# A decoder layer on one core: how the context of a convolution gets reversed and turned

## What is computed

```python
x1 = layernorm(x + linear_attention(x))          # stage 1
# stage 2: k = v = context, q = x1, 512 features in heads of 8, L = positions x features by head
kv  = einsum('bhil,bhjl->bijhl', k_, v_)         # all pairs of a head's 8 rows
y   = irfft(rfft(kv) * rfft(ssm_kernel))[..., :L] + kv * D   # causal convolution along l
out = einsum('bijhl,bhil->bjhl', y, q_)
x2  = layernorm(x1 + out)
# stage 3: 4-bit weights, SiLU gate, 1408 hidden features
x3  = layernorm(x2 + rmsnorm(down(silu(gate(x2)) * up(x2))))
```

## Time and profile before

| what | value |
|---|---|
| device time, 3 runs | median 538.91 us (538.29 to 539.4) |
| the profiled execution's own time | 539.25 us |
| its span in the profile | 537.4 us, 11880 instructions |
| granted TensorE clock over the span | 0.995 of full speed |
| DMA, whole span | 66147 packets, 40.64 MB, mean 76 GB/s |

### The profile page before, as it was taken

How to read it: one execution, slowest core, us unless ns; L and a number is a source line. 1 busy time by engine, 2 the same in 40 slices (tenths; PEclk the granted TensorE clock), 3 DMA queues, 4 the chain that set the end, 5 groups by cost and what they waited for, 6 DMA issues and landing times.

```text
span 537.4 us, 11880 instructions
## 1 busy us (share of the span) xinstructions
PE 512.8 (95%) x3734; PEld 385.9 (72%) x3734; DVE 383.2 (71%) x1169; ACT 405.8 (76%) x962; POOL 393.7 (73%) x449
## 2 busy tenths in 40 slices
PE   6899999998998999999999999999999999999992
PEld 6788888776775678667767776777677767765661
DVE  2897679998787677876778677778777777763223
ACT  3468774338998888878888898889788877788981
POOL 2379694994798499859967995899589949871231
PEclk9999999999999999999999999999999999999998
DMA  9445584705414761132104110411041111001001
GB/s 225 102 119 124 132 169 108 183 1 123 135 53 86 143 132 51 49 86 93 55 7 112 63 59 0 117 59 59 5 116 35 39 29 51 1 1 41 1 21 39
DMA packets 66147, 40.64 MB, mean 76 GB/s; under 512 B 37882, under 2 KB 55418, under 8 KB 66106
## 3 DMA queue, kind: packets, MB, share of 16 engines
q1 hardware_dynamic: 66106, 40.13, 29.5%
HBM read 27.46 MB, written 12.66 MB: 75 GB/s over the span
## 4 chain that ended last, share of the span: by engine, by line
PE 44%; POOL 28%; issue 18%; DVE 4%; ACT 3%; POOLq 1%; DMA 1%; DVEq 0%; ACTq 0%
POOL shared L295 9%; POOL h_lo L1103 6%; PE p_qk L901 5%; POOL kv L195 3%; PE p_cv L867 3%; PE p_cv L135 3%; PE p_n L1296 3%; PE p_n L1294 3%; PE p_n L1295 3%; PE p_cv L137 3%; PE p_cv L136 3%; POOL shared L297 2%; PE p_n L912 2%; PE p_x L1281 2%; PE p_n L957 2%
## 5 line engine op out<-in xcount | busy, mean ns | idle before, releaser
L1103 POOL TENSOR_TENSOR h_lo<-w,h_hi 128x256 f16<-128x256 f32 x88 | 70.5, 807 | 46.9 <-ACT h_hi L1152 45.4
L135 PE MATMUL p_cv<-kv_hi,toe 128*128 128x288 f16 x320 | 91.6, 286 | 0.8 <-DVE shared L255 0.8
L136 PE MATMUL p_cv<-kv_lo,toe 128*128 128x288 f16 x320 | 91.5, 286 | 0.0
L137 PE MATMUL p_cv<-kv_hi,toe 128*128 128x288 f16 x320 | 91.5, 286 | 0.0
L1135 ACT ACTIVATE p_qk<-p_qk,rescale 128x256 f32<-128x256 f32 x192 | 78.3, 450 | 12.9 <-PE p_qk L1283 12.3
L1135 ACT ACTIVATE p_x<-p_x,rescale 128x256 f32<-128x256 f32 x192 | 78.4, 452 | 8.1 <-PE p_x L1283 8.0
L295 POOL TENSOR_TENSOR shared<-shared 128x1024 f32<-128x1024 f32 x32 | 75.5, 2360 | 4.9 <-DVE shared L255 4.9
L1135 ACT ACTIVATE p_s<-p_s,rescale 128x256 f32<-128x256 f32 x144 | 58.9, 455 | 10.9 <-PE p_s L1283 10.9
L1294 PE MATMUL p_n<-wd_hi,h_hi 128*128 128x512 f16 x176 | 66.8, 379 | 0.0
L1296 PE MATMUL p_n<-wd_hi,h_lo 128*128 128x512 f16 x176 | 66.7, 379 | 0.0
L1295 PE MATMUL p_n<-wd_lo,h_hi 128*128 128x512 f16 x176 | 66.7, 379 | 0.0
(11 more groups left out here) (170 smaller groups left out, 1283.7 us busy)
## 6 DMA issues: line engine op xcount, KB each, us to landing
toe<-toeplitz_rows SPq DMA_DIRECT2D x16, 512.0 KB, 3.7
cnat<-in_ctx SPq DMA_DIRECT2D x16, 256.0 KB
xq<-x_blocks SPq DMA_DIRECT2D x16, 256.0 KB, 6.0
xr<-x_rows SPq DMA_DIRECT2D x16, 256.0 KB
out_x<-fin SPq DMA_DIRECT2D x16, 256.0 KB
ring<-in_x SPq DMA_DIRECT2D x6, 512.0 KB, 4.8
x_rows<-ring SPq DMA_DIRECT2D x6, 512.0 KB, 3.5
x_blocks<-ring SPq DMA_DIRECT2D x48, 64.0 KB
```

The costliest lines, as they stand in the source:

```text
L135: nc.tensor.matmul(dst, hi, kh, start=(mb == 0), stop=False)
L136: nc.tensor.matmul(dst, hi, kl, start=False, stop=False)
L137: done = nc.tensor.matmul(dst, lo, kh, start=False, stop=(mb == lb))
L1103: nc.gpsimd.tensor_tensor(h_lo[:, i, :], h32[:, i % 2, :], h_hi[:, i, :], ALU.subtract).then_inc(h_low, 1)
```

## The change

- The context is copied once, early in the program, from its input into a second tensor in DRAM, `ctx_quarters`, in quarters of its columns (32 of every 128), batches grouped by parity. These are 40 DMAs from DRAM to DRAM, ten steps `cr0` to `cr9` of four on SP's queue (`quarter_ctx`); their runs are 32 numbers (128 bytes) long. Steps cr0 to cr3 bring 32 positions each of one parity, cr4 to cr9 bring 64.
- `cnat` is loaded from `ctx_quarters` with four DMAs of 64 KB in place of one of 256 KB (`load_ctx`, step `cx`). It waits until the copy steps of its positions have landed.
- ScalarE's steps `rv` and `ct`/`kt` and TensorE's step `ct`/`f` go. VectorE's new step `ct`/`kt` (`turn_ctx`) turns `cnat` in 32x32 blocks, read backwards, into `kT`.
- x1 is stored in quarters too: four DMAs a tile in place of eight, with runs of 32 numbers as before; `xq` is loaded in rows of 512 numbers instead of four rows of 128. `turn_q` writes in another pattern.
- All tables of the start and of the periods are new.

```diff
+def load_quarters(sp, dst, quarters, row, signal):
+    src = quarters[:, bass.ds(row, 16)].rearrange("f s e c x -> f (s e) (c x)")
+    sp.dma_start(dst[:], src).then_inc(signal, 16)
+
+def load_ctx(sp, dst, quarters, row, signal):
+    for c in range(4):
+        src = quarters[:, :, c, bass.ds(row, 16)].rearrange("f e s x -> (f e) s x")
+        sp.dma_start(dst[:, c * P:(c + 1) * P], src).then_inc(signal, 16)
...
+    def turn(dst, src, order, first, step):
+        return nc.vector.transpose(
+            bass.AP(dst.tensor, dst.offset, [list(dst.ap[0]), [16, 16]] + order),
+            bass.AP(src.tensor, src.offset + first, [list(src.ap[0]), [32, 4], [P, 4], [step, 32]]))
...
-        nc.vector.transpose(cv.qv[p][:].rearrange("p (e r j) -> p r e j", e=2, j=8),
-                            cv.xq[p][:].rearrange("p (b k c) -> p k b c", k=KD, c=32)).then_inc(cv.q_kept, 1)
+        turn(cv.qv[p][:], cv.xq[p][:], [[256, 2], [1, 8], [8, 2]], 0, 1).then_inc(cv.q_kept, 1)
+
+    def turn_ctx(g, p):
+        dve.wait_ge(cv.in_ctx[p], (g + 1) * 64)
+        wait(dve, cv.kv_made, (g - 1) * HG + 2 * p + 2)
+        turn(cv.kT[p][:], cv.cnat[p][:], [[8, 2], [256, 2], [1, 8]], 31, -1).then_inc(cv.kT_kept, 1)
...
+        def quarter_ctx(n):
+            r, e = n // 2, n % 2
+            rows = (slice(0, 32), slice(32, 64), slice(64, 128), slice(128, 192), slice(192, 256))[r]
+            for f in range(LB):
+                sp.dma_start(ctx_quarters[f, e, :, rows, :].rearrange("b s (k c) -> b s k c", c=32),
+                             ctx_in[e::2, rows, :].rearrange("b s (k f c) -> f b s k c", f=4, c=32)[LB - 1 - f]
+                             ).then_inc(ctx_quartered[r], 16)
...
             elif name == "cx":
-                sp.wait_ge(cv.ctx_reversed, i - 1)
-                load_ctx(g, p)
+                sp.wait_ge(ctx_quartered[(0, 1, 2, 2)[g]], 128)
+                if g > 0:
+                    sp.wait_ge(cv.kT_kept, i - 1)
+                load_ctx(sp, cv.cnat[p], ctx_quarters, g * 32 + p * 16, cv.in_ctx[p])
...
-    START_SYNC = ("cx2 x3 cx3 x4 st0 st1 tw0 x5 x6 st2 toe0 st3 cx4 xq0 xq1 xq3 toe1 xr0 x7 xq2 cx6 xr1 toe2 xr3 cx5 "
-                  "st4 xq5 toe3 xq4 xr2 toe4 st5 cx7 toe5 st6 st7").split()
+    START_SYNC = ("x3 cr0 cr1 cx1 cx0 cr2 x4 cr3 cx2 cr4 st0 tw0 x5 st1 toe0 toe1 x6 st2 st3 x7 xq0 cr5 xq2 xr0 xq1 "
+                  "toe2 st4 xq3 cx4 xr1 xq4 cr6 cx3 toe3 xr3 st5 cx6 cx5 cr7 xr2 xq5 cr8 toe4 toe5 st6 st7 cr9 cx7").split()
```

More of the change, by code:

```diff
@@ L153, in flip_x2 @@
         done.then_inc(cv.x2_flipped, 1)
-    return bank_after, flip_ctx, convolve, flip_r, flip_x2
+    return bank_after, convolve, flip_r, flip_x2
 def conv_on_scalar(nc, act, cv):
[L160 to L173, removed]
     def high_kv(g, h):
@@ L367, in first_stage @@
     in_x = [sem(f"in_x{k}") for k in range(RING)]
-    x1_blocked = [sem(f"x1_blocked{k}") for k in range(RING)]
+    x1_quartered = [sem(f"x1_quartered{k}") for k in range(RING)]
+    ctx_quartered = [sem(f"ctx_quartered{k}") for k in range(5)]
     x1_stored = [sem(f"x1_stored{k}") for k in range(RING)]
@@ L402, in load_x @@
             wait(sp, x1_stored[i % RING], 16 * (i // RING))
[L403 removed]
+            wait(sp, x1_quartered[i % RING], 64 * (i // RING))
             sp.dma_start(ring[i % RING][:], tokens(x, i)).then_inc(in_x[i % RING], 16)
@@ L408, in store_x1 @@
             sp.dma_start(tokens(x1_rows, i), ring[i % RING][:]).then_inc(x1_stored[i % RING], 16)
[L409 to L418, removed]
+            for f in range(LB):
+                sp.dma_start(x1_quarters[f, P * (i // 4):P * (i // 4) + P, :, i % 4].rearrange(
+                    "s e (k c) -> s e k c", c=32),
+                             ring[i % RING][:].rearrange("p e (k f c) -> p e k f c", f=4, c=32)[:, :, :, f]).then_inc(
+                    x1_quartered[i % RING], 16)
+        def quarter_ctx(n):
+            r, e = n // 2, n % 2
+            rows = (slice(0, 32), slice(32, 64), slice(64, 128), slice(128, 192), slice(192, 256))[r]
+            for f in range(LB):
+                sp.dma_start(ctx_quarters[f, e, :, rows, :].rearrange("b s (k c) -> b s k c", c=32),
+                             ctx_in[e::2, rows, :].rearrange("b s (k f c) -> f b s k c", f=4, c=32)[LB - 1 - f]
+                             ).then_inc(ctx_quartered[r], 16)
         def load_toe(g, p):
             sp.dma_start(cv.toe[p][:], rows[g * 2 + p:g * 2 + p + 1]).then_inc(cv.in_toe[p], 16)
-        def load_blocks(g, p):
-            sp.dma_start(cv.xq[p][:].rearrange("p (b c) -> p b c", b=4),
-                         x1_blocks[2 * g + p].rearrange("b p c -> p b c")).then_inc(cv.in_xq[p], 16)
         def load_rows(dst, signal, g, p):
@@ L446, in on_sync @@
                      dn_packed.rearrange("(t p) c -> p t c", p=P)).then_inc(in_pd, 16)
-        for p in range(2):
-            load_ctx(0, p)
         load_x(2)
@@ L488, in on_sync @@
             step(s)
+        for n in (3, 4):
+            sp.wait_ge(ctx_quartered[n], 128)
         for i in range(4, SLOTS):
             sp.wait_ge(x1_stored[i % RING], 16 * (i // RING + 1))
-            sp.wait_ge(x1_blocked[i % RING], 128 * (i // RING + 1))
+            sp.wait_ge(x1_quartered[i % RING], 64 * (i // RING + 1))
     def on_pool(pool):
@@ L1007, in on_tensor, with periods @@
         return step
-    free = [(sq_made, SLOTS), (xT_kept, 2 * SLOTS), (oT_kept, SLOTS), (z_made, 2 * SLOTS), (x1_blocked[3], 128),
-            (x1_blocked[4], 128)]
+    free = [(sq_made, SLOTS), (xT_kept, 2 * SLOTS), (oT_kept, SLOTS), (z_made, 2 * SLOTS), (x1_quartered[3], 64),
+            (x1_quartered[4], 64)]
     return (on_sync, on_tensor, on_vector, on_scalar, on_pool), free
-def periods(nc, sb, sem, keep, cv, bank, free, ctx_in, toeplitz_rows, x1_rows, x1_blocks, out):
+def periods(nc, sb, sem, keep, cv, bank, free, ctx_in, toeplitz_rows, x1_rows, x1_quarters, ctx_quarters, out):
     ident, halfneg = keep["ident"], keep["halfneg"]
@@ L1076, in body @@
                 if nxt and ctx:
-                    sp.wait_ge(cv.ctx_reversed, it * 2 + 2 + p + 1)
-                    load_ctx(it + 2, p)
+                    sp.wait_ge(cv.kT_kept, it * 2 + 2 + p + 1)
+                    load_ctx(sp, cv.cnat[p], ctx_quarters, (it + 2) * 32 + p * 16, cv.in_ctx[p])
             if late:
@@ L1432, in decoder_layer @@
         first, free = first_stage(nc, sb, sem, keep, cv, bank, x, ctx_2048, w_q, w_k, w_v, w_o, gate, M, z, ssm_kernel,
-                                  ssm_d, gu_packed, gu_scales, dn_packed, dn_scales, toeplitz_rows, x1_rows, x1_blocks)
-        rest = periods(nc, sb, sem, keep, cv, bank, free, ctx_2048, toeplitz_rows, x1_rows, x1_blocks, out)
+                                  ssm_d, gu_packed, gu_scales, dn_packed, dn_scales, toeplitz_rows, x1_rows, x1_quarters,
+                            ctx_quarters)
+        rest = periods(nc, sb, sem, keep, cv, bank, free, ctx_2048, toeplitz_rows, x1_rows, x1_quarters, ctx_quarters, out)
         with nc.Block() as block:
@@ L1446, in _ @@
                 step, body = first[1](pe, flips), rest[1](pe, flips)
-                last = [s for s in PE_ORDER if s[:2] in ("ct", "rt", "xt")][-1]
+                last = [s for s in PE_ORDER if s[:2] in ("rt", "xt")][-1]
                 run(pe, step, lambda it, order: body(it, order, last if len(order) > 1 else None), START_PE, PE_ORDER,
```

99 lines of the change are left out of this document (41 added, 58 removed), and 47 rows, old and new, of tables (PE_ORDER, START_ACT, START_DVE, START_PE).

## The result

The change makes the kernel slower: 586.44 us (median of 4 runs, 585.56 to 587.91) against 538.78 us (538.29 to 539.4) for the kernel before on the same chip, a ratio of 1.0879, 95% interval 1.0853 to 1.0906. The forecast was 578.0 with a range of 538 to 625. The profiled execution took 586.85 us, its span 585.1 us.

What follows compares the result with a forecast made beforehand. The prediction took TensorE to bound the periods, and a chain across engines with transfers on one queue the start. It summed 539.25 + 43 (waits) - 4.4 (TensorE's turns) = 577.9, said 578 us, range 538 to 625.

Steps and rivals of the forecast that it cites:

- TensorE's turns: Periods 2 to 6, bound by TensorE: ten groups of four turns go, 0.44 us each, saving 4.4 us.
- ScalarE, SP's issues in the periods, VectorE's turns at no cost: Periods: ScalarE's removed copies, SP's 4.3 us more of issues and VectorE's 1.4 to 2.4 us of turns each change nothing.
- my bound of 0.95: VectorE's new turns, the query's too: at most 0.95 us each, from 0.69 x 1.38.
- A run costs one engine 14.2 ns: Copy DMAs: each 128-byte run occupies one DMA engine for 14.2 ns, taken from the store of `x_blocks`.
- the bounds of 5.7 and 38: Time of a copy run on one DMA engine: 5.7 ns from large rows, 38 ns from the mean of all packets.
- The sign I named: Profile after: a DMA share near 0.25 at about 36 GB/s while a copy step runs alone.
- First wait: First tile: the context turn ahead of `o` waits for cr0 and cr1 and the context loads; TensorE's next step 21 us later.
- Second wait: Second half's query: its load stands behind copy steps up to cr5, so terms 8 come 33 us late.
- Third wait: Up to period 2: cr6 to cr8 stand ahead of context, Toeplitz and query loads; period 2 starts 43 us late in all.
- the 12 us that I allowed for idle engines: Load sum up to period 2: the first four DMA engines idle at least 12 us because a landing is waited for.
- The wide copy: Rival: copy spreads over 16 engines, later waits vanish, first wait of +8 to +10 us remains; 540 to 542 us; chance 0.12.
- The wait is taken up: Rival at the turn ahead of `o`: wide copy, `cnat0` landed before about 27 us, wait covered; 532 us; chance 0.09.

Runs made afterwards that it cites:

- experiment 2: Changed kernel with the same 40 copy DMAs walked with rows (128 or 256) outermost and the four quarters inside: 545.46 us, ratio 1.0138 to before.
- experiment 5: Changed kernel with the copy walked with 8 batches outermost, as many DMAs and runs: 551.07 us, ratio 1.0242 to before.
- experiment 4: Changed kernel without any copy, context loaded straight from the input in four pieces, tables and turns unchanged: 536.76 us, ratio 0.9969 to before.
- Experiment 6: On top of experiment 3, the query turn writes in the context turn's quick pattern: 535.63 us, ratio 0.9936 to before; period still 50.91 us.
- Experiment 8: Wide copy, later first turn, x1 stored in eight pieces a tile, plus the kernel before's period orders adapted to the moved turns: 539.4 us, ratio 1.0008.
- experiment 1: Changed kernel, narrow copy kept, with the first context turn and POOL's first pair products moved later: 585.04 us, ratio 1.0888 to before.
- experiment 3: Changed kernel with both the copy walked rows outermost and the first context turn and pair products later: 536.35 us, ratio 0.9963 to before.

## Why the prediction was right, and where it missed

The mechanism held, and its condition too: four outermost, a copy at the pace of few engines, waits at a context turn, at the query, and up to period 2. The experiments show it from both sides (2 and 5 change only the walk of the DMAs, 4 removes them). The forecast of 578 is 8.4 us low. That it is so near is in part luck: up to terms 8 it was 9.5 us too high, from there to period 2 it was 16.3 us too low. Term by term:

- **TensorE's turns, -4.4 us in periods 2 to 6.** Mis-sized: -2.1 us from period 2 to the end. A period fell by 0.29 us (51.20 to 50.91), where eight turns' worth 0.88. I took TensorE as the only bound of a period; with its queue shorter, steps of POOL, ScalarE and VectorE hold it at three places for the other 0.58 us. Experiment 6 excludes the slow query turn as cause. Experiment 8 shows that the old tables are worse; whether a third order would give more no run shows.
- **ScalarE, SP's issues in the periods, VectorE's turns at no cost.** Held: with no copy the kernel isn't slower than before (experiment 4). In the old order one turn a period held TensorE (experiment 8), so VectorE's slack covers the turns only where they are placed well. A context turn took 0.70 us as taken; a query turn 1.07 us, above my bound of 0.95, scaled from a pair of products that differ by less.
- **A run costs one engine 14.2 ns.** It was 11.4 ns, within the bounds of 5.7 and 38. The row of the x1 store was the right neighbour, but 14.2 is 25% too dear, because I took the share for a count of engines (0.59 x 16 = 9.4). With eight engines for the 8 groups of that store, which the pace of experiment 5 suggests, the same row says 8 / 664 = 12.0 ns. The sign I named, a share of 0.25 at 36 GB/s, was 0.40 at 43, for the same reason. The upper bound of 38 ns stood on a wrong remark too: 37882 of the 66147 packets before are under 512 bytes, so most don't carry far more bytes than a run.
- **First wait, +21 us.** Measured +14.0: 2.9 us from the pace (1024 runs an engine at 2.8 ns less), some 2 because cr0 and cr1 had the engines from about 18 us (landed by 29.5, less 1024 x 11.4 ns) where I had put 20, and the rest because SP saw the landing sooner than my 1 us and a load issued in 0.64 in place of 0.72. But as a term the first wait was read wrongly: experiment 1 shows that it isn't additive. My reason was right only for a wide copy, 9.1 us in experiment 3, where I had put +8 to +10 for that rival.
- **Second wait, 33 us at terms 8.** Measured 23.5 us, of which the stall behind cr5 is 9.05.
- **Third wait, +43 us in all at period 2.** Measured +49.8, so from terms 8 on 26.3 us, where I had 10. A run was cheaper than in my sum, so the 12 us that I allowed for idle engines, because landings are waited for, were far too few. Between terms 8 and period 2 SP waits for no landing, but for buffers that others have still to free (us in total, times, longest; and the window of the first wait):

```profile
SPq L483 <- DVE qv L209: 13.1, 1, 13.1
SPq L465 <- DVE kT L209: 8.7, 1, 8.7
...
130.97:144.21 13.24, 12.32 (x91) 10.57 (x89) 11.81 (x39) 5.12 (x10) 11.08 (x9) 1.00 0.13 43
```

5.6 us for x1 come to it. The queue runs empty (a share of 0.13), and cr6 behind it starts only at 144.79; the context load of the third stall stands behind cr6 in turn. In the kernel before SP waits even longer between 101 and 184 us, 50.6 us, but no copy stands behind. Nor had I that a copy step holds SP itself for 12.6 us. And the clock's term was missing: up to 9.2 us of TensorE's time behind terms 8 went at the 1.2 GHz level. How much of it lay on the path I can't say.
- **Rivals.** The wide copy exists, by experiment, at 545.5 where I had put 540 to 542: the first wait as forecast, but 4.4 + 2.6 us off TensorE were worth 2.1. "The wait is taken up" needed the landing at 27 us; in experiment 2 it came at 28.7 and cost 8.16 us, and only with the turn moved are wait and loss gone, at 536.35 and not 532.

## What to carry to other kernels

A copy that nobody waits for can still set the end: if its DMAs use few engines, everything behind them on the same queue is late. While the copy was narrow, moving the first instruction that waits for it only moved the wait. SP's own waits for buffers stand in the same order, so a copy step behind such a wait starts late and ends late. Look at the walk of a DMA before its bytes: with rows instead of batches outermost the same runs were worth 41 us here. And when work moves to an engine with slack, look at where it stands in that engine's order, and expect the relieved engine to meet other engines' steps: 0.58 of 0.88 us went to them here.
